# A GNN and mixture-of-experts layer on one core: the down matrices become the moving side of their matmuls, and x1 accumulates with tokens on partitions

## The chip, the cores and the metric

The kernel runs on one core of a Trainium2 chip. The metric is the device time of one execution in microseconds (us), as the median of repeated runs. A shorter time is better.

## The reference

Of one layer with 96 tokens of 1024 features, this case touches the last part. x1 is the input plus a graph attention branch plus a linear attention branch. Then x1 gets a feed-forward part in f32 and bf16, with 8 experts of which a token uses 2:

```
scores = sigmoid(xf @ gate_w.T);  sel = top_k(scores + expert_bias, 2)
h = (xf * score_of_e).astype(bf16) @ w_up[e].T.astype(bf16)      # 1024 -> 1408
h = square(relu(h.astype(bf16)))
routed_out = (h @ w_down[e].T.astype(bf16)).astype(bf16)         # 1408 -> 1024
hs = square(relu(xf @ shared_w_up.T))                            # f32
out = x1 + sum over experts of routed_out + hs @ shared_w_down.T
```

xf is the layer norm of x1. The weights lie in f32 in HBM. An expert has 5.77 MB of up weights and 5.77 MB of down weights.

## The kernel before, in words

The kernel computes every expert for all 96 tokens and gives a token the weight 0 where it isn't routed. It has no planner: each engine's order is written out by hand, and semaphores join them.

**The first part** (to about 183 us) runs the eleven 1024x1024 matrices of the two attention branches. They come in pieces of 1 MB through five slots of a buffer named `ring`. TensorE (PE) multiplies them in `out_transposed` (L822: the weights are the stationary side, the tokens move) or in `out_rows` (L835: 96 tokens are stationary, 512 weight columns move). At its end VectorE (DVE) has x1 in `acc`, with tokens on partitions (L684). TensorE transposes x1 into banks 0 and 1 (L804 with `acc`), ScalarE (ACT) copies that to `acc_t` (L395), and TensorE transposes the normalised rows in the same way (L804 with `xn`).

**The second part** is the feed-forward. `expert(e, ...)` at L958 does one expert on TensorE. Its up product (L976) keeps 128x128 blocks of up weights stationary and moves the 96 tokens, 88 matmuls in three groups (`TILES`). ScalarE applies relu (L420) and VectorE squares (L737) into `e_h`, which holds hidden features on partitions and tokens in its columns. The down product (L993) does the same with down weights: for each of 8 output tiles of 128 features, 11 matmuls over the hidden features, with 96 columns moving. They are cut by `OUT_TILES` into three groups of 3, 3 and 2 output tiles, and group j writes bank j. After a group, ScalarE rounds the bank to bf16 (L433, into `rounded`), VectorE adds that to `acc_t` (L753), and after the last expert SyncE (SP) stores the group (L292). So `acc_t` and the output hold features on partitions.

The shared expert runs in f32. Its up product (L947) lies between the parts of experts 0 and 1, its down product (L1020) between expert 1 and expert 2. Its weights go through `ring`, by SP's queue (L283 and L287), while all expert weights come by GpSimd's queue (POOL, L302).

**The loads of the experts.** Three buffers `stage[0..2]` hold one expert each, and a load turns f32 in HBM into bf16 in SBUF. An expert has six loads: three of up weights and three of down weights, cut as the groups of matmuls are. Expert e uses `stage[e % 3]`. The loads of experts 0 to 2 are issued between the pieces of the first part. From expert 3 on, POOL waits for the group of matmuls that used that place (`up_done`, `down_done` of expert e - 3), in order, and issues the load:

```
for e in range(3, EXPERTS):
    for j in range(PARTS):
        pool.wait_ge(up_done, up_before(e - 3) + j + 1)
        load(e, 0, j)
    for j in range(PARTS):
        pool.wait_ge(down_done, down_before(e - 3) + j + 1)
        load(e, 1, j)
```

The last load is issued at about 283 us, and the last 80 us wait only for transfers that are queued.

Of the kernel before, what the change touches and what calls it, by code (L numbers as in the profile page):

```python
# [18 lines left out]
P = 128  # L19
# [26 lines left out]
DUNIT = TT * P  # L46
TILES = [(0, 4), (4, 8), (8, 11)]
OUT_TILES = [(0, 3), (3, 6), (6, 8)]
# [17 lines left out]
def gps_layer(nc, x, mats, bias_v, bias_o, ln_gamma, ln_beta, edge_rows, columns, shared_up, shared_down, expert_up, expert_down, out):  # L66
    ctx = ExitStack()
    with ctx:
# [22 lines left out]
        def sh_dn(o, t):  # L91
            return ring[:, o * DUNIT + t * P:o * DUNIT + (t + 1) * P]

# [32 lines left out]
        rounded = acc[:, 0:KT * N // 2].bitcast(BF16)  # L126
# [91 lines left out]
        x1t_psum = sem("x1t_psum")  # L218
        x1t_ready = sem("x1t_ready")
# [50 lines left out]
        @block.sync  # L270
        def _(sp):
            sp.dma_start(xs[0:N, 0:D], x).then_inc(x_landed, 16)

            for piece in range(SLOTS):
                load_piece(sp, piece)

            for j in range(SLOTS + 1):
                if j < SLOTS:
                    pieces_used(sp, len(STEPS) * PIECES - SLOTS + j + 1)
                else:  # L280
                    sp.wait_ge(pre_ready, 1)
                f0, f1 = j * PIECE, min((j + 1) * PIECE, BUF)
                sp.dma_start(ring[:, f0:f1], shared_up[:, f0:f1]).then_inc(sh_up_landed[j], 16)  # L283
            for j, (o0, o1) in enumerate(OUT_TILES):
# [5 lines left out]
            for j, (o0, o1) in enumerate(OUT_TILES):  # L290
                sp.wait_ge(added, EXPERTS * PARTS + j + 1)
                sp.dma_start(out[:, o0 * N:o1 * N], acc_t[:, o0 * N:o1 * N])\  # L292
                  .then_inc(out_landed, 16)
            sp.wait_ge(out_landed, 16 * PARTS)

        @block.gpsimd
        def _(pool):
            def load(e, m, j):
                b = e % 3
                f0, f1 = [(t * UNIT, o * DUNIT)[m] for t, o in zip(TILES[j], OUT_TILES[j])]  # L300
                place = stage[b].rearrange("p (m n) -> p m n", m=2)[:, m, :].bitcast(BF16)
                pool.dma_start(place[:, f0:f1], (expert_up, expert_down)[m][e, :, f0:f1])\  # L302
                    .then_inc(stage_landed[b][PARTS * m + j], 16)
# [35 lines left out]
        def _(act):  # L339
# [71 lines left out]
            def expert(e, between=None, late=None):  # L411
# [13 lines left out]
                for j, (o0, o1) in enumerate(OUT_TILES):  # L425
# [7 lines left out]
                    nc.scalar.activation(rounded[:, o0 * N:o1 * N], bank[j][:, 0:(o1 - o0) * N],  # L433
# [9 lines left out]
        def _(dve):  # L443
# [302 lines left out]
            def add(e, before):  # L746

                for j, (o0, o1) in enumerate(OUT_TILES):
# [7 lines left out]
            dve.wait_ge(x1t_ready, 2)  # L756
# [10 lines left out]
            for j, (o0, o1) in enumerate(OUT_TILES):  # L767
                dve.wait_ge(down_done, 2 * PARTS + j + 1)
                dve.wait_ge(added, PARTS + j + 1)
                cols = slice(o0 * N, o1 * N)  # L770
                tt(acc_t[:, cols], bank[j][:, 0:(o1 - o0) * N], acc_t[:, cols], ALU.add)\
# [9 lines left out]
        def _(pe):  # L781
# [147 lines left out]
            transpose_rows(acc, 0, x1_ready, x1t_psum)  # L929
# [28 lines left out]
            def expert(e, b, turn, free, between=None, late=None):  # L958
# [7 lines left out]
                down = stage[b][:, TT * UNIT // 2:TT * UNIT].bitcast(BF16)\  # L966
                    .rearrange("p (o t j) -> p o t j", o=KT, t=TT)
# [13 lines left out]
                for j, (o0, o1) in enumerate(OUT_TILES):  # L981
# [32 lines left out]
            for j, (o0, o1) in enumerate(OUT_TILES):  # L1014
# [76 lines left out]
```

## Time and profile before

| what | value |
|---|---|
| median of 3 runs | 364.7 us (364.47 to 365.04) |
| the profiled execution | 363.93 us |
| its span | 362.1 us |
| granted TensorE clock, mean over the span | 0.891 of full speed |
| TensorE busy | 301.4 us, 83% of the span |
| VectorE, ScalarE busy | 30%, 11% |
| read from HBM | 150.48 MB |

The span runs from the first to the last recorded event. The profiled execution took 1.83 us more than its span. A share of busy time says little here: the chain of waits and the rows of the 16 DMA engines must be read beside it, and the last stretch for itself.

### The profile page before, as it was taken

The page shows a single profiled execution, that of the slowest core. Times are in us where ns is not written, and L with a number is a line of the kernel's source. Part 1 is how long each engine was busy: PE and PEld are TensorE (multiplying, and loading weights), DVE is VectorE, ACT ScalarE, POOL GpSimd, SP SyncE. Part 2 cuts the span into 40 slices and gives each one's busy share as a digit, 9 for nine tenths or more (in the row PEclk, how much of TensorE's full clock was granted, in tenths as well). Part 3 has the DMA queues.
Part 4 walks back from the last instruction along what each step waited for, and adds up shares of the span by engine and source line. Part 5 has one row for each costly group of instructions (what it writes and reads, how often), then busy time and mean ns, then how long its engine had stood idle before and what let it go on. Part 6 is the DMA issues. An engine that isn't in the chain of part 4 may idle for free.

```text
span 362.1 us, 6375 instructions
## 1 busy us (share of the span) xinstructions
PE 301.4 (83%) x2808; PEld 242.5 (67%) x2808; DVE 107.9 (30%) x249; ACT 39.5 (11%) x81; POOL 51.8 (14%) x95
## 2 busy tenths in 40 slices
PE   5999999999999999999369999599998555544644
PEld 4999999998343343433149999599888554543543
DVE  7608605410070657303334330100243111011001
ACT  1400000000004010300030221000122101001010
POOL 0511212111212312110110221000133100000000
PEclk9999999999999999999887999889999855566566
DMA  8999999999999999999999999999999999999993
GB/s 301 359 297 389 341 318 416 309 346 418 322 313 414 355 309 387 351 347 309 342 295 279 239 213 265 322 323 269 214 215 216 214 216 216 216 213 216 215 214 92
DMA packets 15298, 105.07 MB, mean 290 GB/s; under 512 B 1712, under 2 KB 2248, under 8 KB 4524
## 3 DMA queue, kind: packets, MB, share of 16 engines
q0 software_dynamic: 12528, 87.04, 88.0%
q1 hardware_dynamic: 2560, 17.56, 12.0%
q8 instruction: 18, 0.29, 0.3%
q10 hardware_dynamic: 188, 0.14, 0.1%
q14 instruction: 4, 0.03, 0.0%
HBM read 150.48 MB, written 0.39 MB: 417 GB/s over the span
## 4 chain that ended last, share of the span: by engine, by line
PE 67%; DMA 23%; another core or an unknown queue 5%; DVE 2%; issue 1%; ACT 1%; ACTq 0%
PE bank L822 21%; PE bank L835 20%; DMA stage<-in_expert_up 14%; PE bank L976 6%; PE bank L1020 6%; PE bank L993 6%; DMA ring<-in_mat_wo 5%; PE bank L947 4%; DMA ring<-in_shared_down 4%; PE bank L789 1%; PE bank L936 1%; PE bank L804 1%; PE bank L1005 0%; PE bank L880 0%
## 5 line engine op out<-in xcount | busy, mean ns | idle before, releaser
L993 PE MATMUL bank<-hbuf,stage 128*128 128x96 bf16 x704 | 40.8, 229 | 21.2 <-DMA stage<-in_expert_down 18.7
L835 PE MATMUL bank<-ring,xnt 128*96 128x512 f32 x128 | 55.5, 593 | 0.0
L976 PE MATMUL bank<-late,stage 128*128 128x96 bf16 x704 | 39.4, 225 | 18.9 <-DMA stage<-in_expert_up 17.8
L993 PEld LDWEIGHTS bank<-hbuf,stage 128*128 128x128 bf16 x704 | 38.5, 112 | 23.4 <-issue 15.9
L976 PEld LDWEIGHTS bank<-late,stage 128*128 128x128 bf16 x704 | 37.1, 109 | 20.8 <-issue 16.6
L822 PE MATMUL bank<-xnt,ring 128*128 128x96 f32 x384 | 46.6, 287 | 0.6 <-ACT xnt L352 0.6
L822 PEld LDWEIGHTS bank<-xnt,ring 128*128 128x128 f32 x384 | 46.3, 204 | 1.0 <-ACT xnt L352 0.9
L835 PEld LDWEIGHTS bank<-ring,xnt 128*96 128x96 f32 x128 | 20.7, 163 | 33.1 <-issue 33.0
L822 PE MATMUL bank<-stage,ring 128*128 128x96 f32 x256 | 28.8, 275 | 0.0
L822 PEld LDWEIGHTS bank<-stage,ring 128*128 128x128 f32 x256 | 28.7, 192 | 0.0
L1020 PE MATMUL bank<-xs,ring 128*128 128x96 f32 x176 | 22.5, 296 | 3.6 <-DMA ring<-in_shared_down 3.6
L1020 PEld LDWEIGHTS bank<-xs,ring 128*128 128x128 f32 x176 | 22.3, 212 | 3.8 <-issue 3.8
L302 POOL DMA_DIRECT2D stage<-in_expert_up x24 | 12.9, 537 | 77.1 <-PE bank L976 54.6
L753 DVE TENSOR_TENSOR acc_t<-acc,acc_t 128x288 f32<-128x288 bf16 (+1 forms) x24 | 10.0, 425 | 43.6 <-ACT acc L433 43.6
L737 DVE TENSOR_TENSOR hbuf<-xn 128x384 bf16<-128x384 bf16 (+1 forms) x24 | 8.2, 342 | 49.5 <-ACT xn L420 49.5
L947 PE MATMUL bank<-xnt,ring 128*128 128x96 f32 x176 | 22.5, 291 | 0.0
L947 PEld LDWEIGHTS bank<-xnt,ring 128*128 128x128 f32 x176 | 21.9, 207 | 0.0
L835 PE MATMUL bank<-ring,acc_t 128*96 128x512 f32 x32 | 15.8, 646 | 5.6 <-DMA ring<-in_mat_wo 5.6
L420 ACT ACTIVATE xn<-bank 128x384 bf16<-128x384 f32 (+1 forms) x24 | 11.1, 463 | 72.8 <-PE bank L976 72.8
L302 POOL DMA_DIRECT2D stage<-in_expert_down x24 | 12.8, 534 | 37.7 <-PE bank L993 28.3
L835 PEld LDWEIGHTS bank<-ring,acc_t 128*96 128x96 f32 x32 | 5.6, 180 | 14.9 <-issue 8.4
L539 DVE TENSOR_TENSOR stage<-bank,cols 128x384 f32<-128x384 f32 x10 | 5.4, 555 | 33.2 <-PE bank L822 33.2
(154 smaller groups left out, 199.3 us busy)
## 6 DMA issues: line engine op xcount, KB each, us to landing
stage<-in_expert_down POOLq DMA_DIRECT2D x16, 1056.0 KB, 34.0
stage<-in_expert_up POOLq DMA_DIRECT2D x16, 1024.0 KB, 21.6
stage<-in_expert_up POOLq DMA_DIRECT2D x8, 768.0 KB, 25.1
stage<-in_expert_down POOLq DMA_DIRECT2D x8, 704.0 KB, 39.8
ring<-in_shared_up SPq DMA_DIRECT2D x5, 1024.0 KB, 16.5
ring<-in_shared_down SPq DMA_DIRECT2D x2, 2112.0 KB, 14.4
ring<-in_mat_wq SPq DMA_DIRECT2D x4, 1024.0 KB, 9.2
ring<-in_mat_wv POOLq DMA_DIRECT2D x4, 1024.0 KB, 9.4
```

Of the source, the lines that this page charges most:

```text
L302: pool.dma_start(place[:, f0:f1], (expert_up, expert_down)[m][e, :, f0:f1])\
L420: nc.scalar.activation(e_relu[:, t0 * N:t1 * N], bank[4 + j][:, 0:(t1 - t0) * N], ACT.Relu).then_inc(relu_done, 1)
L539: tt(tiles(dst)[:, h * HT:(h + 1) * HT, :], tiles(bank[BANKS[m] + h][:, 0:HT * N]), b, ALU.add).then_inc(half_out, 1)
L737: tt(e_h[:, t0 * N:t1 * N], r, r, ALU.mult).then_inc(h_ready, 1)
L753: tt(acc_t[:, cols], rounded[:, cols], acc_t[:, cols], ALU.add)\
L789: ins = mm(bank[KEY_BANKS[r]][:, g * P:(g + 1) * P], pick[:, at:at + 1].broadcast_to([EC, P]), ends_r[:, end * P:(end + 1) * P], start=(en ...
L822: ins = mm(bank[BANKS[m] + h][:, at * N:(at + 1) * N], w[:, k, o * P:(o + 1) * P], tiles(src)[:, k, :], start=(k == 0), stop=(k == KT - 1))
L835: ins = mm(bank[BANKS[m] + h][0:N, :], tiles(src)[:, k, :], w[:, kk, :], start=(k == 0), stop=(k == KT - 1))
L947: ins = mm(bank[SHARED_BANKS[j]][:, (t - t0) * N:(t - t0 + 1) * N], sh_up_t[:, t, k, :], tiles(xnt[:])[:, k, :], start=(k == 0), stop=(k = ...
L976: ins = mm(bank[4 + j][:, (t - t0) * N:(t - t0 + 1) * N], up[:, t, k, :], tiles(xe)[:, k, :], start=(k == 0), stop=(k == KT - 1))
L993: ins = mm(bank[j][:, (o - o0) * N:(o - o0 + 1) * N], down[:, o, t, :], tiles(e_h)[:, t, :], start=(t == 0), stop=(t == TT - 1))
L1020: ins = mm(bank[j][:, (o - o0) * N:(o - o0 + 1) * N], sh_dn(o, t), tiles(sh_h)[:, t, :], start=(t == 0), stop=(t == TT - 1))
```

## The change

The down product of each expert, and of the shared expert, is turned round. The squared up product (`e_h` or `sh_h`, 128 hidden features by 96 tokens) is now stationary, and the down weights move, in blocks of 512, 384 and 128 output columns (`OUT_COLS`). A block is 11 matmuls, one for each tile of hidden features. Per expert 88 matmuls with 96 moving columns become 33 with 512, 384 or 128. The result has tokens on partitions. So x1 itself, `acc`, accumulates, and the transposes of x1 and their copies go. `rounded` moves from `acc` to `acc_t`. The down weights are laid out by block on the host, and a load covers one block: 5632, 4224 and 1408 f32 numbers of each partition in place of 4224, 4224 and 2816. The output is stored as rows of tokens.

```diff
-OUT_TILES = [(0, 3), (3, 6), (6, 8)]
+OUT_COLS = [(0, 512), (512, 896), (896, 1024)]
...
-        rounded = acc[:, 0:KT * N // 2].bitcast(BF16)
+        rounded = acc_t[0:N, 0:HALF].bitcast(BF16)
...
-                sp.dma_start(ring[:, o0 * DUNIT:o1 * DUNIT], shared_down[:, o0 * DUNIT:o1 * DUNIT])\
+                sp.dma_start(ring[:, c0 * TT:c1 * TT], shared_down[:, c0 * TT:c1 * TT])\
...
-                sp.dma_start(out[:, o0 * N:o1 * N], acc_t[:, o0 * N:o1 * N])\
+                sp.dma_start(out[:, c0:c1], acc[0:N, c0:c1])\
...
-                f0, f1 = [(t * UNIT, o * DUNIT)[m] for t, o in zip(TILES[j], OUT_TILES[j])]
+                f0, f1 = [(t * UNIT, c * TT)[m] for t, c in zip(TILES[j], OUT_COLS[j])]
...
-                act.wait_ge(x1t_psum, b + 1)
-                nc.scalar.activation(acc_t[:, b * GROUP * N:(b + 1) * GROUP * N],
-                                     bank[b][:, 0:GROUP * N], ACT.Copy).then_inc(x1t_ready, 1)
-            for b in range(2):
...
-                    nc.scalar.activation(rounded[:, o0 * N:o1 * N], bank[j][:, 0:(o1 - o0) * N],
+                    nc.scalar.activation(rounded[:, c0:c1], bank[j][0:N, 0:c1 - c0],
...
-                    cols = slice(o0 * N, o1 * N)
-                    tt(acc_t[:, cols], rounded[:, cols], acc_t[:, cols], ALU.add)\
+                    tt(acc[0:N, c0:c1], rounded[:, c0:c1], acc[0:N, c0:c1], ALU.add)\
...
-            transpose_rows(acc, 0, x1_ready, x1t_psum)
+            pe.wait_ge(x1_ready, 2)
...
-                    elif j < 2:
-                        pe.wait_ge(x1t_ready, j + 1)
                     if j == 0:
                         pe.wait_ge(h_ready, up0 + PARTS)
-                    for o in range(o0, o1):
-                        for t in range(TT):
-                            ins = mm(bank[j][:, (o - o0) * N:(o - o0 + 1) * N], down[:, o, t, :],
-                                     tiles(e_h)[:, t, :], start=(t == 0), stop=(t == TT - 1))
+                    w = down[:, c0 * TT:c1 * TT].rearrange("p (t c) -> p t c", t=TT)
+                    for t in range(TT):
+                        ins = mm(bank[j][0:N, 0:c1 - c0], tiles(e_h)[:, t, :], w[:, t, :],
+                                 start=(t == 0), stop=(t == TT - 1))
                     ins.then_inc(down_done, 1)
...
-                for o in range(o0, o1):
-                    for t in range(TT):
-                        ins = mm(bank[j][:, (o - o0) * N:(o - o0 + 1) * N], sh_dn(o, t),
-                                 tiles(sh_h)[:, t, :], start=(t == 0), stop=(t == TT - 1))
+                w = ring[:, c0 * TT:c1 * TT].rearrange("p (t c) -> p t c", t=TT)
+                for t in range(TT):
+                    ins = mm(bank[j][0:N, 0:c1 - c0], tiles(sh_h)[:, t, :], w[:, t, :],
+                             start=(t == 0), stop=(t == TT - 1))
                 ins.then_inc(down_done, 1)
...
+    def by_columns(w):
+
+        w = w.reshape(D, TT, P).transpose(2, 1, 0)
+        return np.concatenate([w[:, :, c0:c1].reshape(P, -1) for c0, c1 in OUT_COLS], axis=1)
```

Two places show how the instructions move. The first is TensorE in the loop over the later experts, the down product of one that uses `stage[1]`, as the last expert does. Before:

```order
L986 REGISTER_ALU [waits stage_landed1_3]
L990 REGISTER_ALU [waits out_taken]
L993 MATMUL bank<-hbuf,stage 128x96 [waits h_ready]
L993 MATMUL bank<-hbuf,stage 128x96 x32
L986 REGISTER_ALU [waits stage_landed1_4]
L993 MATMUL bank<-hbuf,stage 128x96 [waits out_taken]
L993 MATMUL bank<-hbuf,stage 128x96 x32
L993 MATMUL bank<-hbuf,stage 128x96 [waits out_taken,stage_landed1_5]
L993 MATMUL bank<-hbuf,stage 128x96 x21
```

Now (the line numbers are those of the changed kernel, where L977 is the down product):

```order
L972 REGISTER_ALU [waits stage_landed1_3]
L974 REGISTER_ALU [waits out_taken]
L977 MATMUL bank<-stage,hbuf 96x512 [waits h_ready]
L977 MATMUL bank<-stage,hbuf 96x512 x10
L972 REGISTER_ALU [waits stage_landed1_4]
L977 MATMUL bank<-stage,hbuf 96x384 [waits out_taken]
L977 MATMUL bank<-stage,hbuf 96x384 x10
L977 MATMUL bank<-stage,hbuf 96x128 [waits out_taken,stage_landed1_5]
L977 MATMUL bank<-stage,hbuf 96x128 x10
```

The waits are the same three, one ahead of each group (`stage_landed1_3` to `_5` are the landings of the three down loads). What stands behind each is 11 matmuls of falling width in place of 33, 33 and 22 of equal width.

The second is POOL, which issues the loads of one later expert. Before:

```order
L302 DMA stage<-in_expert_up 128x4096 [waits up_done] x2
L302 DMA stage<-in_expert_up 128x3072 [waits up_done]
L302 DMA stage<-in_expert_down 128x4224 [waits down_done] x2
L302 DMA stage<-in_expert_down 128x2816 [waits down_done]
```

Now:

```order
L296 DMA stage<-in_expert_up 128x4096 [waits up_done] x2
L296 DMA stage<-in_expert_up 128x3072 [waits up_done]
L296 DMA stage<-in_expert_down 128x5632 [waits down_done]
L296 DMA stage<-in_expert_down 128x4224 [waits down_done]
L296 DMA stage<-in_expert_down 128x1408 [waits down_done]
```

The number of loads, their order and what each waits for stay; the three down loads have other sizes with the same sum.

## Rows read from the trace of the kernel before

**Rows 1.** The page, parts 2 and 3: 40 equal slices, and HBM traffic.

```profile
PEclk9999999999999999999887999889999855566566
DMA  8999999999999999999999999999999999999993
HBM read 150.48 MB, written 0.39 MB: 417 GB/s over the span
```

**Rows 2.** Stretches: us; PE, PEld, DVE, ACT, POOL busy; PEclk, DMA share, GB/s.

```profile
220.00:250.00 30.00, 26.37 (x251) 26.25 (x249) 2.02 (x5) 1.64 (x4) 1.58 (x3) 0.89 1.02 311
256.00:356.00 100.00, 61.12 (x1015) 57.35 (x1012) 18.07 (x40) 14.51 (x34) 9.49 (x18) 0.70 1.02 213
350.00:355.00 5.00, 2.90 (x37) 2.69 (x36) 0.46 (x1) 0.41 (x1) 0.00 (x0) 0.50 0.93 197
```

**Rows 3.** The chain that ended last: start us, length us, what.

```profile
218.91 14.39 DMA ring<-in_shared_down
...
323.03 2.82 PE bank L993 x33
...
343.79 0.84 another core or an unknown queue
...
345.94 3.67 another core or an unknown queue
...
349.83 2.82 PE bank L993 x33
352.65 1.98 another core or an unknown queue
...
354.75 2.82 PE bank L993 x33
357.57 0.58 another core or an unknown queue
...
358.19 1.12 PE bank L993 x22
...
359.76 0.36 DVE acc_t L753
```

**Rows 4.** Timeline of POOL: start us, us, instruction, idle time before it and releaser.

```profile
202.09 0.53 POOL L302 DMA_DIRECT2D stage<-in_expert_up  x1 [17.95 <-PE bank L976]
257.55 0.53 POOL L302 DMA_DIRECT2D stage<-in_expert_up  x1 [26.92 <-PE bank L976]
```

**Rows 5.** Timeline of PE, the same columns (an f32 matmul is two records).

```profile
57.38 1.06 PE L856 MATMUL bank<-stage 128*96 128x96 bf16 x20
...
154.73 13.90 PE L835 MATMUL bank<-ring,xnt 128*96 128x512 f32 x32
...
186.41 0.91 PE L804 MATMUL bank<-ident,xn 96*128 96x96 f32 x8 [2.29 <-DVE xn L691]
...
233.44 22.45 PE L1020 MATMUL bank<-xs,ring 128*128 128x96 f32 x176 [3.63 <-DMA ring<-in_shared_down]
...
314.26 2.74 PE L976 MATMUL bank<-late,stage 128*128 128x96 bf16 x32 [2.08 <-DMA stage<-in_expert_up]
```

**Rows 6.** Stretches of 1 us (the last two of PE alone: busy, PEclk, DMA, GB/s).

```profile
238.00:239.00 1.00, 1.00 (x7) 1.00 (x7) 0.00 (x0) 0.00 (x0) 0.00 (x0) 0.65 0.98 315
...
317.00:318.00 1.00, 0.09 (x3) 0.89 1.04 217
...
358.00:359.00 1.00, 0.81 (x19) 0.91 0.00 1
```

**Rows 7.** Groups by line and shape: busy us, mean ns of one, idle time before.

```profile
L420 ACT ACTIVATE xn<-bank 128x384 bf16<-128x384 f32 x16 | 7.8, 490 | 64.3 <-PE bank L976 64.3
L433 ACT ACTIVATE acc<-bank 128x192 bf16<-128x192 f32 x8 | 2.6, 330 | 7.0 <-PE bank L993 7.0
...
L539 DVE TENSOR_TENSOR stage<-bank,cols 128x384 f32<-128x384 f32 x10 | 5.4, 555 | 33.2 <-PE bank L822 33.2
...
L753 DVE TENSOR_TENSOR acc_t<-acc,acc_t 128x192 f32<-128x192 bf16 x8 | 2.9, 358 | 5.3 <-ACT acc L433 5.3
```

More of the change, by code:

```diff
@@ L283, in _ @@
                 sp.dma_start(ring[:, f0:f1], shared_up[:, f0:f1]).then_inc(sh_up_landed[j], 16)
-            for j, (o0, o1) in enumerate(OUT_TILES):
+            for j, (c0, c1) in enumerate(OUT_COLS):
                 sp.wait_ge(up_done, up_before(2) - (j == 0))
-                sp.dma_start(ring[:, o0 * DUNIT:o1 * DUNIT], shared_down[:, o0 * DUNIT:o1 * DUNIT])\
+                sp.dma_start(ring[:, c0 * TT:c1 * TT], shared_down[:, c0 * TT:c1 * TT])\
                   .then_inc(sh_dn_landed[j], 16)
-            for j, (o0, o1) in enumerate(OUT_TILES):
+            for j, (c0, c1) in enumerate(OUT_COLS):
                 sp.wait_ge(added, EXPERTS * PARTS + j + 1)
-                sp.dma_start(out[:, o0 * N:o1 * N], acc_t[:, o0 * N:o1 * N])\
+                sp.dma_start(out[:, c0:c1], acc[0:N, c0:c1])\
                   .then_inc(out_landed, 16)
@@ L423, in expert @@
                     shared_relu(between, up0 + PARTS + 1)
-                for j, (o0, o1) in enumerate(OUT_TILES):
+                for j, (c0, c1) in enumerate(OUT_COLS):
                     if not isinstance(e, int):
@@ L746, in add @@
             def add(e, before):
-                for j, (o0, o1) in enumerate(OUT_TILES):
+                for j, (c0, c1) in enumerate(OUT_COLS):
                     dve.wait_ge(out_taken, e * PARTS + (j + 1))
@@ L765, in _ @@
             add(1, 0)
-            for j, (o0, o1) in enumerate(OUT_TILES):
+            for j, (c0, c1) in enumerate(OUT_COLS):
                 dve.wait_ge(down_done, 2 * PARTS + j + 1)
                 dve.wait_ge(added, PARTS + j + 1)
-                cols = slice(o0 * N, o1 * N)
-                tt(acc_t[:, cols], bank[j][:, 0:(o1 - o0) * N], acc_t[:, cols], ALU.add)\
+                tt(acc[0:N, c0:c1], bank[j][0:N, 0:c1 - c0], acc[0:N, c0:c1], ALU.add)\
                     .then_inc(added, 1)
@@ L965, in expert @@
                     .rearrange("p (t k j) -> p t k j", t=TT, k=KT)
-                down = stage[b][:, TT * UNIT // 2:TT * UNIT].bitcast(BF16)\
-                    .rearrange("p (o t j) -> p o t j", o=KT, t=TT)
+                down = stage[b][:, TT * UNIT // 2:TT * UNIT].bitcast(BF16)
                 up0 = up_before(e)
@@ L980, in expert @@
                     shared_up(between)
-                for j, (o0, o1) in enumerate(OUT_TILES):
+                for j, (c0, c1) in enumerate(OUT_COLS):
                     if late is not None and j == PARTS - 1:
@@ L1013, in _ @@
             pe.wait_ge(h_ready, up_before(2))
-            for j, (o0, o1) in enumerate(OUT_TILES):
+            for j, (c0, c1) in enumerate(OUT_COLS):
                 pe.wait_ge(out_taken, PARTS + j + 1)
                 pe.wait_ge(sh_dn_landed[j], 16)
-                for o in range(o0, o1):
-                    for t in range(TT):
-                        ins = mm(bank[j][:, (o - o0) * N:(o - o0 + 1) * N], sh_dn(o, t),
-                                 tiles(sh_h)[:, t, :], start=(t == 0), stop=(t == TT - 1))
+                w = ring[:, c0 * TT:c1 * TT].rearrange("p (t c) -> p t c", t=TT)
+                for t in range(TT):
+                    ins = mm(bank[j][0:N, 0:c1 - c0], tiles(sh_h)[:, t, :], w[:, t, :],
+                             start=(t == 0), stop=(t == TT - 1))
                 ins.then_inc(down_done, 1)
@@ L1071 @@
         .reshape(P, TT * UNIT)
-    arrays["shared_down"] = g["L0_ffn_shared_w_down"].reshape(KT, P, TT, P).transpose(3, 0, 2, 1)\
-        .reshape(P, TT * UNIT)
+    arrays["shared_down"] = by_columns(g["L0_ffn_shared_w_down"])
     arrays["expert_up"] = g["L0_ffn_w_up"].reshape(EXPERTS, TT, P, KT, P).transpose(0, 4, 1, 3, 2)\
         .reshape(EXPERTS, P, TT * UNIT)
-    arrays["expert_down"] = g["L0_ffn_w_down"].reshape(EXPERTS, KT, P, TT, P)\
-        .transpose(0, 4, 1, 3, 2)\
-        .reshape(EXPERTS, P, TT * UNIT)
+    arrays["expert_down"] = np.stack([by_columns(w) for w in g["L0_ffn_w_down"]])
     arrays = {f"in_{k}": np.ascontiguousarray(v) for k, v in arrays.items()}
@@ L1083 @@
            for k, a in arrays.items()}
-    out = nc.dram_tensor("out", (P, KT * N), mb.dt.float32, kind="ExternalOutput").ap()
+    out = nc.dram_tensor("out", (N, D), mb.dt.float32, kind="ExternalOutput").ap()
     mat_aps = {k[4:]: aps.pop(k) for k in list(aps) if k.startswith("mat_")}
@@ L1087 @@
     r = run_bass_kernel_spmd(nc, [arrays], core_ids=[0])
-    return np.ascontiguousarray(r.results[0]["out"].reshape(P, KT, N).transpose(2, 1, 0))\
-        .reshape(N, D)
+    return np.ascontiguousarray(r.results[0]["out"])
```

6 lines of the change are left out of this document (removed).

## The prediction

> **What bounds the kernel now.** I read the row of the DMA engines first. It is at 9 tenths in every slice but the first and the last, while TensorE's clock row drops to 5 and 6 tenths in the last quarter, which a TensorE that sets the pace would not show [rows 1]. Over the stretch of 100 us before 356 the engines' share is 1.02 at 213 GB/s written, and a load reads two bytes for each that it writes, so some 426 GB/s are read; TensorE is busy for 61 us of the 100 [rows 2]. The whole kernel reads 150.48 MB [rows 1].
>
> The chain says the same of its last part. Its waits for "another core or an unknown queue" stand exactly where the next group of matmuls waits for its load, so they are landings. The last up load of expert 7 landed at 343.79 + 0.84 = 344.63, its three down loads at 349.61, 354.63 and 358.15 [rows 3]. From the start of one expert's down product to the next expert's is 349.83 - 323.03 = 26.80 us for 11.53 MB read, or 430 GB/s: the stream doesn't pause for anything that TensorE does [rows 3].
>
> Is it ever short of work earlier? I count back from 358.15 in steps of 26.80: the stream comes to the loads of expert 7 at 331.35, of 6 at 304.55, of 5 at 277.75, of 4 at 250.95 and of 3 at 224.15. The shared down weights (5.77 MB, 13.4 us at 430 GB/s) go somewhere before that, so the first load of expert 3 is reached at about 210.8 at the earliest. It was issued at 202.09 and the first of expert 5 at 257.55 [rows 4]. The queue has 8.7 us and 20 us of other work ahead of them. So **the transfers bound the time to 358.15, and only what follows the last landing belongs to the engines**: 22 matmuls, ScalarE's rounding, VectorE's add to 360.12, the store to 362.1 [rows 3].
>
> **Loads.** Per expert there are still six, in the same order on POOL, with the same bytes. The three down loads covered 3/8, 3/8 and 2/8 of the columns and now 1/2, 3/8 and 1/8. A fixed cost of one load, if there were any, would be paid as often as before. I take 0 for the stream. The bounds: the down loads of expert 7 took 358.15 - 344.63 = 13.52 us, half of 26.80 is 13.40, and these loads have other sizes than the up loads, so the size moves the stream by no more than 0.12 us per expert either way, 1 us over 8. Landings of expert 7 become 344.63 + 6.76 = 351.39, then 356.46, and again 358.15.
>
> **The matmuls, first where they are hidden.** No bf16 matmul with 512 moving columns stands in the trace. The nearest rows bound it. In f32, 16 of them take 13.90 us, about 864 ns each [rows 5], or four cycles of 2.4 GHz a column. In bf16, 33 matmuls of 96 columns took 2.82 us at 0.50 of the clock [rows 3], 85 ns each or 43 at full clock, which is one cycle a column and a little. So bf16 at 512 columns costs a quarter of the f32 row, 216 ns, or 512/96 of the narrow one, 228 ns. I take 216, 162 and 57 ns for 512, 384 and 128 columns, since the f32 row has the same width and the same 96 stationary columns. That is 4.8 us for the 33 against 88 x 43 ns = 3.8 at full clock, 1.0 us more per expert, 8 in all; with 228 it would be 1.3 more. All of it but the end lies beside the stream. The shared down product is 11 x (864 + 648 + 216) = 19.0 us, with the slow start of before (5.2 us at half clock, below) 21.6 against 22.45 [rows 5]. Its first load grows by a third, so what took 14.39 us takes 19.2 [rows 3]; with 1 us from expert 0 it starts near 239.3 and ends near 260.9, 5 us later than 233.44 + 22.45 = 255.89 of before. What stands behind it is the up product of expert 2 and then POOL, which waits for it to issue expert 5 at 257.55 + 5; the stream wants that at 277.75, so 15 of 20 us are left. If that cover were gone, each us would count.
>
> **Transposes and copies of x1.** TensorE then waits 2.29 us for VectorE before the transposes of `xn` [rows 5], so the 8 transposes of x1 (1 us, by the 0.91 of the 8 of `xn`) filled idle time, and the two copies of ScalarE too. Worth 0 at 186 us, and anyway under the stream.
>
> **The end, step by step.** The block of 512 starts at 351.39 + 0.22 = 351.61 (before, landing to start was 0.22). The clock is at 0.50 then, 1.2 GHz: 432 ns each, 4.75 us if it stays, to 356.36. The block of 384 lands at 356.46 and starts at 356.58. So at either clock level the first block costs nothing. What the clock is from there decides. Rows show it rising to 2.4 GHz 5.2 us after unbroken work began at 233.44 [rows 5, 6], near 317.2, 3.0 us after the start of the burst at 314.26 [rows 5, 6], and near 358.2, 3.4 us after the start of the burst at 354.75 [rows 3, 6]. From 351.61 that gives 354.6 to 356.8, in the first block or just behind it. So: 384 columns 11 x 162 = 1.78 us to 358.36, 128 columns 11 x 57 = 0.63 to 358.99, against 359.31 before. ScalarE starts 0.09 later; 128 columns cost 277 ns (330 for 192, less 64 at 0.83 ns, from 490 for 384), to 359.36. VectorE waits for its own add of the block of 384: rounding to 358.94, add of 555 ns to 359.53 [rows 7]. Then the last add, 291 ns (358 less 64 at 1.03 ns): 359.83, against 360.12. The store is three row groups with half the bytes in the last, issued by a queue that has just issued the one before; I take the same 1.98 us. **Sum: -0.3 us.** The profiled execution of 363.93 becomes 363.6; it lay 0.8 under the median of 364.7, so the median becomes 364.4.
>
> **A row against a rule.** A bf16 matmul with 96 stationary and 96 moving columns stands once in the trace: 20 of them in 1.06 us, less 0.21 for the last one's own length, are 45 ns apart [rows 5], hardly more than the 43 with 128 stationary columns. So 96 stationary columns don't bind at 128 moving ones. The Trainium skill, "TensorE: Matmul & The Clock Gate", section "Weight-path perf modes — Fast Weight Load (FWL) and DoubleRow", says otherwise: the quick load of the stationary side wants 128 of them and not f32, so this change would lose it; with that page's 1 ns for 1.2 columns a load of 96 takes an estimated 80 ns. By that rule the last block would take 11 x 80 ns = 0.88 us in place of 0.63, of which 0.17 vanish in VectorE's wait for its own add, and the median would be 364.5.
>
> **The rivals.**
> (a) *The clock stays at 1.2 GHz to the end*: slower. The 384 block then takes 3.56 us to 360.14, the last 1.25 to 361.39, 2.08 later than before; with the shorter rounding and add, +2.0 us: **366.7**. Each us of half clock from 356.58 on costs 0.5, so it decides the sign from a rise at 358.6 on, 7.0 us after the first block began. For it: the clock was at 0.50 from 350 to 355 [rows 2]. Against: three bursts of at most 2.8 us with pauses made it rise before. 8%.
> (b) *The weight loads bind in the narrow block*: the nearest row that could is f32 with 128 stationary columns, 22.45 / 176 = 128 ns a record with its slow start [rows 5]. 11 x 128 ns = 1.41 us in place of 0.63, up to +0.8 on the forecast less the 0.17 that VectorE waits anyway: 365.0. The page's rule is this rival with a smaller price.  Still no change that can be measured. 8%, from the 45 ns against it.
> (c) *The stream changes its rate*, since longer runs per partition (22.5 KB) and a layout with other addresses meet HBM otherwise. 350 us would do for 150.48 MB at 430 GB/s, the stream had 357, so a few us exist. An upper bound is the 1 us of the loads' paragraph above, taken with some more for the middle, where SP's and POOL's loads mix at 311 GB/s written [rows 2]: 1.2 us faster, **363.5**, or slower, 365.9. 12% and 7%.
> (d) *The change doesn't reach the end at all*: TensorE is late from the middle because of the 5 us and 1.05 per expert. It needs 8.6 us per expert at full clock and 17 at half in a stream of 26.8, so it catches up by expert 5. 1%.
> The rest, 64%, is my forecast: 364.4, its own range 364.0 to 364.9.
>
> **How the numbers follow.** A measurement of this kernel tells about 0.2%, 0.7 us, from no change, so "faster" is below 364.0 and "slower" above 365.4. Faster: 12% from (c) and 4% from the forecast's lower edge, 0.16. Slower: (a) 8%, (c) 7% and 1%, 0.16. The same: 0.68. The range leaves out (a) and the outer part of (c): 363.5 to 365.8.
>
> **What the profile of the changed kernel would show.** DMA share 1.0 to the end and 26.8 us from one expert's down product to the next; landings of the last expert 1.7 us apart at the end; blocks of 512 start at PEclk 0.50; the last 11 matmuls in 0.6 to 0.7 us, at 0.9 or more of the clock, starting after the last landing or within 0.2 us of it; the shared down product starting 5 to 6 us later. Wrong would be: a gap of DMA share between 200 and 280 us, a last block behind a cold 384 block, or 26.8 turned into another number.

## The result and the profile after

The changed kernel took 362.99 us (median of 8 runs, 362.69 to 363.56) beside 364.19 us for the kernel before on the same chip (8 runs). The ratio is 0.9968, with a 95% interval of 0.9959 to 0.9977: **faster by 1.2 us**, where 364.4 us in a range of 363.5 to 365.8 was forecast. That forecast was 0.3 us down from 364.7, the median of the first three runs of the kernel before, which over eight runs is 364.19. Traced once more in the experiments it came out at 0.9968 again (0.9956 to 0.9979). The profiled execution took 362.69 us with a span of 360.9 us, so it lost 1.2 us of span against the 362.1 of before as well.

The page of the changed kernel, part 2, reads as before: the DMA engines are full to the end, and TensorE's clock is lower in the last quarter, though less so [rows 1].

```profile
PEclk9999999999999999999887999969999978558868
DMA  7999999999999999999999999999999999999994
HBM read 150.48 MB, written 0.39 MB: 418 GB/s over the span
```

The stretches of the changed kernel (us; PE, PEld, DVE, ACT, POOL busy; PEclk, DMA share, GB/s) answer to [rows 2]. The engines' share and the GB/s are those of before, so the transfers still bound it.

```profile
220.00:250.00 30.00, 24.99 (x122) 15.31 (x121) 2.97 (x6) 2.14 (x5) 1.58 (x3) 0.89 1.03 311
256.00:355.00 99.00, 64.72 (x728) 49.59 (x726) 19.00 (x40) 15.09 (x33) 9.50 (x18) 0.79 1.03 214
350.00:355.00 5.00, 4.67 (x11) 2.07 (x11) 0.00 (x0) 0.00 (x0) 0.00 (x0) 0.50 0.89 182
```

The chain that ended last (start us, length us, what) answers to [rows 3]:

```profile
219.88 16.73 DMA ring<-in_shared_down
...
236.75 22.02 PE bank L1004 x66
...
323.50 4.71 PE bank L977 x11
328.21 0.09 another core or an unknown queue
...
341.38 2.02 another core or an unknown queue
...
344.71 5.40 another core or an unknown queue
...
350.33 6.87 PE bank L977 x22
```

The reader is to see two things. From one expert's down product to the next it is 350.33 - 323.50 = 26.83 us, against 26.80 before: the rate of the stream near the end has not changed. But the last up load of expert 7 landed at 341.38 + 2.02 = 343.40, where it landed at 344.63 before [rows 3]. The whole gain is there already. From that landing to the end of the span it is 17.5 us in both kernels. So what was forecast, a shorter end, gave nothing that these two traces can show, and **the stream, on which I had put 0, came 1.2 us earlier**.

TensorE's timeline of the end (start us, us, instruction, idle time before it) prints the three blocks as one row of 33 matmuls, with no wait between them that it counts:

```profile
343.52 1.19 PE L962 MATMUL bank<-late,stage 128*128 128x96 bf16 x24 [2.14 <-DMA stage<-in_expert_up]
350.33 7.47 PE L977 MATMUL bank<-stage,hbuf 128*96 128x512 bf16 x33 [5.62 <-DMA stage<-in_expert_down]
```

To find where the stream gained, I took for each load its issue and its time to landing. I compared the two kernels wherever as many bytes had gone before, after all three down loads of an expert or after an up load. The view rounds the time to landing, so each is good to 0.05 us:

| landing of | before | changed | difference |
|---|---|---|---|
| last down load, expert 0 | 82.01 | 81.87 | -0.1 |
| last piece of `mat_wo` | 177.52 | 177.06 | -0.5 |
| first up load, expert 4 | 254.70 | 254.37 | -0.3 |
| last down load, expert 4 | 276.60 | 276.84 | +0.2 |
| first up load, expert 5 | 281.95 | 281.23 | -0.7 |
| last up load, expert 5 | 291.03 | 289.81 | -1.2 |
| last up load, expert 6 | 317.83 | 316.57 | -1.3 |
| last up load, expert 7 | 344.60 | 343.43 | -1.2 |

In these two traces the gain arises between 277 and 291 us, and it stays. At that time TensorE works through experts that have long landed, and the only queues beside POOL's are two that the page lists as "instruction". The first of them, q8, carried 18 packets before and 15 now (the other, q14, 4 and 5). Before, the 17th of the 18 comes between 276 and 278 us and the 18th between 283 and 285 us. The DMA view of the kernel before for 270 to 275 us (queue and kind: packets, MB, share of 16 engines) shows one of them:

```profile
q0 software_dynamic: 185, 1.05, 102.2%
q8 instruction: 1, 0.02, 1.2%
```

One packet of 16 KB holds 1.2% of 16 engines over 5 us, which is 0.96 us of one engine, while the loads go on beside it. I took a load to be spread over the engines and to have landed when the slowest is done; rows further down bear on that. In every experiment I therefore looked at three things: the number of these packets over the execution, the start of the last up group of expert 7 (which is 0.1 us behind its landing), and the time.

### The profile page after: what moved, and what is told of

It reads as the page before. It is cut to its first block, busy times and chain, and to the rows that moved or that the text cites. A ratio compares the mean times of both kernels' runs of the same rounds, so it can differ in the third digit from the quotient of the medians.

```text
span 360.9 us, 5255 instructions
## 1 busy us (share of the span) xinstructions
PE 302.1 (84%) x2250; PEld 216.9 (60%) x2250; DVE 109.6 (30%) x249; ACT 40.3 (11%) x79; POOL 51.9 (14%) x95
## 4 chain that ended last, share of the span: by engine, by line
PE 64%; DMA 27%; another core or an unknown queue 4%; DVE 2%; issue 1%; ACT 1%; DVEq 0%; ACTq 0%
PE bank L809 20%; PE bank L822 16%; DMA stage<-in_expert_down 13%; PE bank L977 7%; PE bank L1004 6%; PE bank L962 6%; DMA ring<-in_mat_wo 5%; DMA ring<-in_shared_down 5%; DMA ring<-in_mat_mv 4%; PE bank L934 4%; PE bank L776 1%; PE bank L923 1%; PE bank L791 1%; PE bank L989 0%
## 5 line engine op out<-in xcount | busy, mean ns | idle before, releaser
L977 PE MATMUL bank<-stage,hbuf 128*96 128x512 bf16 (+2 forms) x264 | 46.8, 338 | 18.9 <-DMA stage<-in_expert_down 16.4
L977 PEld LDWEIGHTS bank<-stage,hbuf 128*96 128x96 bf16 x264 | 29.1, 132 | 36.3 <-issue 24.0
L962 PE MATMUL bank<-late,stage 128*128 128x96 bf16 x704 | 36.5, 219 | 15.9 <-DMA stage<-in_expert_up 15.3
L809 PE MATMUL bank<-xnt,ring 128*128 128x96 f32 x384 | 45.2, 282 | 0.6 <-ACT xnt L346 0.6
L809 PEld LDWEIGHTS bank<-xnt,ring 128*128 128x128 f32 x384 | 44.8, 199 | 1.0 <-ACT xnt L346 0.9
L962 PEld LDWEIGHTS bank<-late,stage 128*128 128x128 bf16 x704 | 34.8, 105 | 17.1 <-issue 15.3
L1004 PE MATMUL bank<-ring,xs 128*96 128x512 f32 (+2 forms) x66 | 22.0, 499 | 5.0 <-DMA ring<-in_shared_down 5.0
L742 DVE TENSOR_TENSOR acc<-acc_t,acc 96x512 f32<-96x512 bf16 (+2 forms) x24 | 11.5, 507 | 45.2 <-ACT acc_t L423 45.2
L934 PE MATMUL bank<-xnt,ring 128*128 128x96 f32 x176 | 22.8, 294 | 0.0
L934 PEld LDWEIGHTS bank<-xnt,ring 128*128 128x128 f32 x176 | 22.4, 210 | 0.0
L1004 PEld LDWEIGHTS bank<-ring,xs 128*96 128x96 f32 x66 | 10.5, 177 | 16.5 <-issue 16.5
L423 ACT ACTIVATE acc_t<-bank 96x512 bf16<-96x512 f32 (+2 forms) x24 | 10.8, 450 | 53.9 <-PE bank L977 52.9
```

The lines of the kernel that those rows point to most:

```text
L423: nc.scalar.activation(rounded[:, c0:c1], bank[j][0:N, 0:c1 - c0], ACT.Copy).then_inc(out_taken, 1)
L742: tt(acc[0:N, c0:c1], rounded[:, c0:c1], acc[0:N, c0:c1], ALU.add)\
L809: ins = mm(bank[BANKS[m] + h][:, at * N:(at + 1) * N], w[:, k, o * P:(o + 1) * P], tiles(src)[:, k, :], start=(k == 0), stop=(k == KT - 1))
L934: ins = mm(bank[SHARED_BANKS[j]][:, (t - t0) * N:(t - t0 + 1) * N], sh_up_t[:, t, k, :], tiles(xnt[:])[:, k, :], start=(k == 0), stop=(k = ...
L962: ins = mm(bank[4 + j][:, (t - t0) * N:(t - t0 + 1) * N], up[:, t, k, :], tiles(xe)[:, k, :], start=(k == 0), stop=(k == KT - 1))
L977: ins = mm(bank[j][0:N, 0:c1 - c0], tiles(e_h)[:, t, :], w[:, t, :], start=(t == 0), stop=(t == TT - 1))
```

## The experiments

The kernels of one call ran on one chip and share their runs of the kernel before, which had a median of 364.11 us in the first call, 364.00 in the second and 363.99 in the third.

### Sizes of the loads or orientation of the matmuls

The change has two halves that can be made apart. The first two kernels of the first call make one each:

```diff
-OUT_TILES = [(0, 3), (3, 6), (6, 8)]
+OUT_TILES = [(0, 4), (4, 7), (7, 8)]
```

> The kernel before (down weights stationary, x1 transposed) with one edit: its three groups of output tiles are 4, 3 and 1 instead of 3, 3 and 2. So its down loads have the sizes of the changed kernel (1408, 1056 and 352 KB) and nothing else of the change. Theory S (the sizes of the loads make the stream of transfers faster): landings 1.2 us earlier from expert 5 on, 363.0 to 363.5 us, about 0.8 to 1.2 under the kernel before. Theory O (the orientation of the matmuls and the timing that it gives the middle part make it): no change, 364.0 to 364.4, stream as before. Theory N (the difference is one of builds or executions, not of this change): anywhere within 0.5 us of the kernel before.

```diff
-OUT_COLS = [(0, 512), (512, 896), (896, 1024)]
+OUT_COLS = [(0, 384), (384, 768), (768, 1024)]
```

> The changed kernel with blocks of 384, 384 and 256 output columns, so that its loads have the old sizes (1056, 1056 and 704 KB). Everything else of the change stays. Theory S: the stream is as before, last landing near 358.1 us, and the end costs 11 x 108 ns in place of 1.12 us: 364.0 to 364.3 us. Theory O: 363.0 to 363.4 us, as the changed kernel.

The other two of the call are the two kernels unchanged, for the scatter of traces.

> The kernel before, unchanged, built and traced once more, to see how far landings differ between two executions of one kernel. Theories S and O: landings within 0.3 us of the first trace (first load of expert 5 at 281.95, last landing 358.16), time ratio 1.000. Theory N: the first load of expert 5 lands 0.5 us or more away from 281.95, and the time differs by up to 0.5 us.

> The changed kernel, built and traced once more. Theories S and O: last landing within 0.3 us of 356.70, first load of expert 5 within 0.3 us of 281.23, ratio 0.997 again. Theory N: landings off by 0.5 us or more.

The sizes alone gave 363.63 us, a ratio of 0.9988 (0.9976 to 1.0001). The moving side with the old sizes gave 363.41 us, a ratio of 0.9992 (0.9977 to 1.0007); its median is 0.7 us under the kernel before, its ratio is not. By time alone neither theory is chosen: 363.63 lies between the two ranges that were expected. The landings choose. The rows are the q8 line of each kernel's DMA view and TensorE's start on the last up group of expert 7. First the sizes alone (stationary weights, new sizes):

```profile
q8 instruction: 18, 0.29, 0.3%
344.69 1.19 PE L976 MATMUL bank<-late,stage 128*128 128x96 bf16 x24 [0.96 <-DMA stage<-in_expert_up]
```

Then the moving side with the old sizes:

```profile
q8 instruction: 15, 0.25, 0.2%
343.74 1.19 PE L962 MATMUL bank<-late,stage 128*128 128x96 bf16 x24 [2.13 <-DMA stage<-in_expert_up]
```

The kernel before, traced again:

```profile
344.85 2.10 PE L976 MATMUL bank<-late,stage 128*128 128x96 bf16 x24 [0.97 <-DMA stage<-in_expert_up]
```

And the changed kernel, traced again:

```profile
343.66 1.19 PE L962 MATMUL bank<-late,stage 128*128 128x96 bf16 x24 [0.93 <-DMA stage<-in_expert_up]
350.43 8.08 PE L977 MATMUL bank<-stage,hbuf 128*96 128x512 bf16 x33 [5.58 <-DMA stage<-in_expert_down]
```

Traces of one kernel repeat this start within 0.15 us, and the sizes don't move it. Earlier landings scatter more, and one expectation failed by it: in the second trace of the kernel before, the first load of expert 5 landed at 282.5, 0.5 us behind the first trace, which was to be theory N's sign. By the last up load of expert 5 the traces of one kernel agree again, with 291.0 and 291.3 before the change and 289.8 and 289.9 after it. So only rows behind 290 us are compared from here on, and by them theory N falls, and so does theory S, which blamed the sizes. What stands is that something in the orientation moves the stream by 1.1 us. Orientation changes two things at once: what TensorE reads, and how many instructions it has.

### Instructions or data

The next call separates these. Three kernels add matmuls to the changed one, between the up and the down product of each expert from the third (expert 2) on. They write to a bank that nothing reads and leave the result alone.

```diff
+                if not isinstance(e, int):
+                    for _ in range(55):
+                        mm(bank[3][0:32, 0:8], ident[:, :].bitcast(BF16)[:, 0:32],
+                           late_w[:, 0:8], start=True, stop=True)
```

> The changed kernel with 55 tiny matmuls (32 stationary, 8 moving columns, into the unused bank 3) added per expert from expert 2 on, between its up and down products: per expert as many TensorE instructions as before the change (88 down matmuls), and almost no data read. Theory I (an instruction fetch of 16 KB takes one DMA engine some 0.6 us, the loads wait for the slowest engine, and 15 fetches in place of 18 made the last landing earlier): 17 or 18 fetches, the last landing back at 357.9 to 358.4 us, 363.9 to 364.4 us. Theory O (weights as the moving side load SBUF or the DMA engines less): last landing stays at 356.7 to 357.0, time 362.9 to 363.5.

With `range(110)`:

> The same with 110 tiny matmuls per expert. Theory I: 20 fetches, the last landing 1.2 to 1.8 us later than with 55, near 359.5, time near 365.5. Theory O: last landing at 356.7 to 357.0, time 362.9 to 363.8.

With `range(20)` and 96 stationary by 512 moving columns:

> The changed kernel with 20 wide matmuls (96 stationary, 512 moving columns, into the unused bank 3) added at the same place: few instructions (one fetch of 16 KB at most in all), but twice the columns read from SBUF. Theory I: last landing 356.7 to 357.5. Theory O, as far as it is the reading of SBUF: last landing later by 1 us or more. Beside that TensorE's clock should be at full speed when the last expert's block of 512 starts, so that the end is shorter by 0.3 to 1.0 us than the changed kernel's: 362.3 to 362.9 us under theory I.

The fourth goes the other way, from the kernel before:

```diff
+                    nt = TT if isinstance(e, int) else 4
                     for o in range(o0, o1):
-                        for t in range(TT):
+                        for t in range(nt):
```

> The kernel before with the down product of experts 2 to 7 cut from 11 to 4 matmuls for each output tile (it leaves out seven elevenths of the hidden features there): 32 matmuls per expert with stationary down weights, about as many instructions as the changed kernel has. Theory I: 15 or 16 fetches, last landing 356.7 to 357.3 though the weights are still the stationary side. Theory O: last landing 358.0 to 358.4.

The last is the clearest. The weights are still the stationary side, TensorE has about as many instructions as in the changed kernel, and the stream is early. Its 17th packet came only at 359 us, behind all loads. Its last load landed at 357.4, 0.1 us beyond the range that theory I gave and well before theory O's 358.0. The kernel leaves out part of the work, so its time can't be set beside a complete kernel's. It was 363.16 us, a ratio of 0.9979 (0.9969 to 0.9988).

```profile
q8 instruction: 17, 0.28, 0.3%
343.71 1.19 PE L976 MATMUL bank<-late,stage 128*128 128x96 bf16 x24 [0.92 <-DMA stage<-in_expert_up]
```

The wide matmuls left it early too, though they read 10240 moving columns per expert beside the 11264 of the down product: the last up load landed at 343.6, with 15 packets. Time 362.90 us, ratio 0.9976 (0.9965 to 0.9987). So theory O falls, in both directions.

Of the tiny ones, 55 per expert made 16 packets (17 or 18 were expected) and moved nothing, where theory I wanted a later stream. The time was 363.03 us, ratio 0.9971 (0.9959 to 0.9984).

```profile
q8 instruction: 16, 0.26, 0.3%
343.55 2.10 PE L963 MATMUL bank<-late,stage 128*128 128x96 bf16 x24 [0.92 <-DMA stage<-in_expert_up]
```

With 110 there were 17 packets (not the 20 that I expected: the loop's body is fetched once for its two passes, so a matmul in it counts three times and not six), and the stream was 0.7 us later. The time was 363.45 us, ratio 0.9986 (0.9977 to 0.9995).

```profile
q8 instruction: 17, 0.28, 0.3%
344.29 2.10 PE L963 MATMUL bank<-late,stage 128*128 128x96 bf16 x24 [0.96 <-DMA stage<-in_expert_up]
```

So the theory needed mending: with 15 or 16 packets the stream lands alike, and the 17th costs about 0.6 us.

### Where the packets fall, and how many

> The changed kernel with the 55 tiny matmuls per expert, and 128 more of them once, at about 172 us, where TensorE waits for the last piece of the first part anyway: one more 16 KB fetch, early. So far 15 and 16 fetches left the last landing at 356.7 to 357.0 us, 17 put it at 357.45 and 18 at 358.2. Theory R (the count over the whole execution decides, wherever the extra fetch is, since the engines' queues never run empty): 17 fetches, last landing 357.3 to 357.6, 363.3 to 363.6 us. Theory L (only fetches after about 270 us cost): last landing 356.7 to 357.0, 363.0.

> The same early 128 tiny matmuls with 110 per expert. Theory R: 18 fetches, last landing 358.0 to 358.4 as in the kernel before, 363.9 to 364.3 us. Theory L: last landing 357.3 to 357.6 as with 110 alone, 363.3 to 363.6.

The early ones are 128 tiny matmuls, once, ahead of the wait for the last piece of the first part:

```diff
+                    if (m, h, i) == ("wo", 1, 1):
+                        for _ in range(128):
+                            mm(bank[4][0:32, 0:8], ident[:, :].bitcast(BF16)[:, 0:32],
+                               ident[:, :].bitcast(BF16)[:, 0:8], start=True, stop=True)
                     piece_landed(pe, piece)
```

With 55 per expert, the 16 packets that cost nothing became 17, the extra one at 179 us. The stream is late only behind the 17th, at 286 us: the last up load of expert 5 landed at 290.5, and at 289.9 with 55 alone.

```profile
q8 instruction: 17, 0.28, 0.3%
344.25 2.10 PE L967 MATMUL bank<-late,stage 128*128 128x96 bf16 x24 [0.96 <-DMA stage<-in_expert_up]
```

With 110 per expert:

```profile
q8 instruction: 18, 0.29, 0.3%
344.75 1.19 PE L967 MATMUL bank<-late,stage 128*128 128x96 bf16 x24 [0.95 <-DMA stage<-in_expert_up]
```

Both starts are theory R's, and so are the last landings, 357.5 and 358.0. The last one is the changed kernel in all but its number of instructions, and its last up group starts at 344.75, 0.12 behind the landing of 344.63 in the kernel before [rows 3]. The times were 363.60 us, ratio 0.9987 (0.9976 to 0.9997), and 363.70 us, ratio 0.9989 (0.9979 to 1.0000). With that the changed kernel has lost its gain but for 0.3 to 0.4 us. The second time is not what theory R expected: it lies under its 363.9 to 364.3 and over theory L's 363.3 to 363.6.

Two of these kernels, which differ in tiny matmuls alone, show where the late stream loses its time (stretch; PE, PEld, DVE, ACT, POOL busy; PEclk, DMA share, GB/s). First with 55 per expert, 16 packets:

```profile
356.00:356.50 0.50, 0.50 (x5) 0.38 (x4) 0.48 (x1) 0.00 (x0) 0.00 (x0) 1.00 0.31 56
356.50:357.00 0.50, 0.50 (x5) 0.37 (x4) 0.21 (x1) 0.00 (x0) 0.00 (x0) 1.00 0.00 0
```

Then with 110 and 128 early, 18 packets:

```profile
356.00:356.50 0.50, 0.49 (x2) 0.09 (x2) 0.00 (x0) 0.00 (x0) 0.00 (x0) 0.50 0.39 73
356.50:357.00 0.50, 0.50 (x2) 0.34 (x3) 0.00 (x0) 0.49 (x1) 0.00 (x0) 0.50 0.12 23
357.00:357.50 0.50, 0.50 (x3) 0.30 (x2) 0.37 (x1) 0.10 (x1) 0.00 (x0) 0.50 0.09 17
```

With 16 packets all engines are done by 356.5 us. With 18, most are done by then too, but 0.12 and 0.09 of 16 engines, one or two of them, go on, and the last load lands 1.2 us later (358.0 beside 356.8). So a load does land with its slowest engine, and the late stream is a few engines that lag, not all of them.

Ten kernels of the twelve side by side, the second traces of the two kernels themselves among them:

| kernel | q8 packets before the last landing | start on last up group | median us |
|---|---|---|---|
| changed, again | 15 | 343.66 | 363.06 |
| changed, old sizes | 15 | 343.74 | 363.41 |
| with 20 wide matmuls | 15 | 343.69 | 362.90 |
| with 55 tiny | 16 | 343.55 | 363.03 |
| before, short down | 16 | 343.71 | 363.16 |
| with 110 tiny | 17 | 344.29 | 363.45 |
| with 55 and 128 early | 17 | 344.25 | 363.60 |
| before, new sizes | 18 | 344.69 | 363.63 |
| with 110 and 128 early | 18 | 344.75 | 363.70 |
| before, again | 18 | 344.85 | 363.94 |

What is fetched counts, and not what TensorE executes: with 110 tiny matmuls it executes 2 x 2910 instructions, more than the 2 x 2808 of before, and its stream is 0.5 us earlier. The first step lies behind 16, and the core has 16 DMA engines. But packets that go round these engines, one each, would not explain the table: the 18th would fall on another engine than the 17th, and since a load waits for its slowest engine alone, it would cost nothing more. It costs about 0.5 us. The traces don't name the engine of a packet, and no kernel has fewer than 15, so why 16 cost no more than 15, and what the first 15 cost, stays open.

With `range(220)` per expert and none early:

> The changed kernel with 220 tiny matmuls per expert: 19 or 20 fetches. Theories R and L: each fetch beyond the 16th puts the last landing 0.6 us later at most, and less where it falls on another DMA engine than the ones before: last landing between 358.0 and 359.3. A theory without fetches: 356.7 to 357.0. The tiny matmuls take 6 us per expert, so TensorE may start the last block of 512 late and the time says less than the landing.

This one went past what I expected: 383.46 us, a ratio of 1.0548 (1.0520 to 1.0577), and 30 packets in place of 19 or 20. TensorE's timeline shows it standing with "issue" as the reason, that is, with no instruction to run:

```profile
302.08 3.49 PE L968 MATMUL bank<-late,ident 128*32 128x8 bf16 x128 [0.72 <-issue]
308.28 0.62 PE L968 MATMUL bank<-late,ident 128*32 128x8 bf16 x17 [2.71 <-issue]
...
321.26 4.02 PE L963 MATMUL bank<-late,stage 128*128 128x96 bf16 x48 [5.18 <-issue]
```

The last load landed at 359.3 us, 2.6 us late, with 27 of the 30 packets before it. The price per packet is not the same all the way: 24 of them came before the last up load of expert 7, which landed at 344.7, as with 18. The other 18 us are TensorE's: its chain has no wait for a load behind 289 us, and in it "issue" for 2.7, 5.2, 1.8 and 2.6 us, beside the longer work itself. The body of the loop had 3 x (242 + 440) = 2046 TensorE instructions beside its register instructions, against 1386 with 110 tiny matmuls, and its second pass was fetched again: once through the program is 5094 instructions, 19.9 packets of 256, and the body once more makes 27.9, where 30 were counted. No kernel lies between the two sizes of the body. The Trainium skill, "Runtime: NRT & Kernel Launch", section "Instruction fetch mechanics", fits that. It says that TensorE keeps 128 KiB of instructions, 2048 of 64 bytes, refilled over DMA in blocks of 16 KiB, 256 instructions. It also says that fetching is hidden behind the issue of instructions. In this kernel it isn't: on DMA engines that are full, the late loads land by the number of packets (344.75 with 18, 343.55 with 16).

### A version that beats both?

```diff
-OUT_COLS = [(0, 512), (512, 896), (896, 1024)]
+OUT_COLS = [(0, 512), (512, 832), (832, 1024)]
```

> The changed kernel with blocks of 512, 320 and 192 output columns, to shorten the end: the middle block lands 0.8 us earlier and takes 0.3 us less, and the last block, of 11 x 81 ns, waits for its landing at 356.9 in place of for the middle block. Working it out: products done at 357.85 (357.8 and 358.5 in the two traces of the changed kernel), last add done at 358.65 against 358.8 and 359.5. Expected 362.6 to 363.0 us, 0.1 to 0.5 under the changed kernel; no gain if the clock rises only behind 356.5.

It gave 362.74 us, a ratio of 0.9963 (0.9949 to 0.9978), the lowest median of all kernels with the right work, but its interval covers the changed kernel's 0.9968. In its trace the last block waits for its load, as intended:

```profile
350.39 5.81 PE L977 MATMUL bank<-stage,hbuf 128*96 128x512 bf16 x22 [5.58 <-DMA stage<-in_expert_down]
356.94 1.11 PE L977 MATMUL bank<-stage,hbuf 128*96 128x192 bf16 x11 [0.74 <-DMA stage<-in_expert_down]
```

It beats the kernel before. Against the changed kernel the 0.3 us between the medians are not shown.

## Why the prediction was wrong

**The step that failed** is the paragraph on the loads: "I take 0 for the stream", with a bound of 1 us from the sizes of the loads. The stream came 1.2 us earlier. I had looked for what could change it in the loads themselves: their number, bytes and run lengths. These are worth nothing that shows; the kernel with new sizes and stationary weights landed where the kernel before does. What I left out is the traffic that the page lists in its own line, "q8 instruction". The change removes it without mentioning it: fewer matmuls are fewer instructions to fetch, by the same engines that bound the kernel. The count could have been worked out beforehand. Before, TensorE executed 2 x 2808 instructions, and the loop's body of 3 x 352 is in that twice. Once through it is 5616 - 1056 = 4560, or 17.8 blocks of 256. The change makes it 4500 - 726 = 3774, or 14.7. The traces show 18 and 15. That the two packets beyond 16 cost 0.5 to 0.6 us each could not have been known from the trace of before.

**The number** missed by 1.4 us, and not all of that is the step above. Of the 1.4 us between 364.4 and 362.99, 0.5 us is the kernel before, whose median I took from three runs (364.7, and 364.19 over eight), and 0.9 us is the change (0.3 forecast, 1.2 measured).

**Rival (c)**, at 12%, had the right place and sign, a faster stream, and by luck the right price: 1.2 us under the kernel before. Its reason (longer runs, other addresses) is not the cause, since the kernel with the new sizes and the old orientation landed late and the one with the old sizes and the new orientation early. Its 363.5 was that price taken from the 364.7 that was too high.

**What bounds the kernel**: right. The DMA share stayed at 1.0 and the distance of experts at 26.83 us. No gap of the stream appeared between 200 and 280 us.

**The hidden matmuls**: right in size. The groups by shape give TensorE's down product 26.9, 15.7 and 6.2 us for 88 matmuls each at mixed clock, and a whole expert at full clock took 4.98 us with its last matmul's drain, where 4.8 was forecast. The shared down product began at 236.75, not 239.3: its first load, a third larger, took 16.73 us and not 19.2; why its time grew by a sixth only, no run shows. It ended 2.9 us later than before instead of 5, and the first load of expert 5 was issued at 260.43, 16 us before the load ahead of it had landed (276.84).

**The narrow block and the stationary side**: the row was right and the rule would not have been. In the changed kernel 22 matmuls, 11 of 384 and 11 of 128 columns, took 2.60 us at full clock, in the chain:

```profile
328.42 2.60 PE bank L977 x22
```

11 x 162 + 11 x 57 ns is 2.41, and the rest is the drain of the last. With the 80 ns estimated from the Trainium skill's "TensorE: Matmul & The Clock Gate", section "LDWEIGHTS (loading the stationary operand)", for each load of 96 stationary columns it would be 2.85 with the same drain. Rival (b) falls, and with it the fear that the quick load of the stationary side would be missed, for blocks of 128 columns and more.

**The clock**: half right. It rose 4.9 us after the start of the block of 512 in the first trace, in the stretch of 1 us from 355:

```profile
355.00:356.00 1.00, 1.00 (x6) 0.65 (x6) 0.02 (x1) 0.59 (x1) 0.00 (x0) 0.91 0.43 84
```

In the second trace it rose near 356.5, 6.1 us after the start at 350.43, later than the 5.2 that I took for the longest:

```profile
356.00:357.00 1.00, 1.00 (x6) 0.73 (x5) 0.69 (x1) 0.04 (x1) 0.00 (x0) 0.75 0.14 25
```

The block of 512 ended just ahead of the next load in both, as was forecast for 1.2 GHz: its eleven matmuls take 4.7 us from 350.33, to 355.0, and the block of 384 began at 355.20, 0.12 us behind the landing of its load at 355.08. But in the second trace the block of 384 then ran partly at 1.2 GHz, and the whole product took 0.6 us longer (8.08 against 7.47 us in the rows above). Rival (a), a cold end, is thus real in part in some executions. The kernel with the 20 wide matmuls kept the clock at full speed through the whole end and had 362.90 us, no more than 0.2 us under the changed kernel and inside its interval.

**The end**: forecast -0.3 us, and nothing of it in the two first traces, 17.5 us from the last up landing to the end of the span in both. From the last landing (358.15 and 356.79) to the end of the last add it is 1.97 us before and 1.77 now, close to the 1.68 forecast. From there to the end of the span it is 2.0 us before and 2.3 now, where I had taken the same. Roundings and adds had the forecast lengths; these are two of the groups by shape:

```profile
L742 DVE TENSOR_TENSOR acc<-acc_t,acc 96x128 f32<-96x128 bf16 x8 | 2.2, 280 | 0.0
L423 ACT ACTIVATE acc_t<-bank 96x128 bf16<-96x128 f32 x8 | 2.2, 272 | 1.0
```

What I missed is SP. The last add began at 358.3 and ended at 358.6, but the add of 384 had ended only 0.2 us before, and SP was issuing that block's store. The issue of the last store began only at 358.76 and took 0.42 us, beside 0.33 before:

```profile
358.76 0.42 SPq L286 DMA_DIRECT2D out<-acc  x1
```

The medians leave something for the end all the same: at equal numbers of packets (18) the changed kernel with its extra matmuls had 363.70 us, 0.3 under the kernel before. That is within what such a comparison can show, and no more than that.

## What to carry to other kernels

In a kernel that is bound by its loads, count every byte that goes over the DMA engines, the instructions too. The page lists them under their own queue, and in this kernel their number followed the TensorE instructions of the program, a loop's body counted once, in packets of 256. A layout with wide moving sides and fewer matmuls can then pay though TensorE itself gets slower, and a part that is "hidden" has a price for what is fetched to run it. Where all loads wait for the slowest of 16 engines, a single small packet on one engine can delay all of them, so look at landings at equal bytes, in two traces of the same kernel first, and then compare.

## What the runs showed of the hardware that was not expected

- With 15 or 16 packets of instructions the loads landed alike. The 17th and 18th cost 0.5 to 0.6 us each, wherever the extra ones fell (at 179 us or at 292 us), and with 24 the landing was no later than with 18. One of 16 KB holds its DMA engine for 0.96 us, beside loads.
- A late stream was one or two DMA engines of 16 that still worked in its last microsecond, when the others were done.
- A loop of 2046 TensorE matmul and weight load instructions was fetched again in its second pass (30 packets, 18 us of waits on TensorE). One of 1386 was not.
- Twenty more matmuls with 512 moving columns per expert, 10240 columns beside the 11264 of the down product, moved the late landings by less than 0.2 us: here TensorE's reading of SBUF didn't slow the loads.
- The clock took from 4.9 to 6.1 us of unbroken work to rise in two executions of one kernel.
